# Window attention with a mixture of experts on one core: ScalarE puts the score biases of pairs 1 to 7 into PSUM, and VectorE rounds the third expert

## The chip, the cores and the metric

One core of a Trainium2 chip runs the whole program. The metric is device time in microseconds (us); lower is better. The kernel before has a median of 6585.76 us over 3 runs (6585.39 to 6585.8).

## The reference

The input `x` is 32 images of 56 x 56 tokens with 96 channels. Each image goes through a layer norm, then attention in shifted windows of 7 x 7 tokens (49 tokens, 12 heads of 8 channels), and a residual. Then come a second layer norm and a mixture of 4 experts (96 to 384 to 96, exact gelu, the best 2 of 4 by a softmax gate), and a second residual. The part that the change touches is the bias of the scores and the hidden layer of the experts:

```python
attn = einsum('bhwnqd,bhwnkd->bhwnqk', q, k) * (1.0 / sqrt(hd))
attn = attn + bias        # rel_table[index], one 49 x 49 table per head
attn = attn + mask        # -inf between the two sides of the shift:
                          # last window row and last window column
p = softmax(attn)
...
h = gelu(einsum('bsd,edh->ebsh', x, w1) + b1)
y = einsum('ebsh,ehd->ebsd', h, w2) + b2
```

## The kernel before, in words

The work is cut into 128 units: 4 for each of the 32 images. A unit is two strips of 7 rows by 56 columns, 784 tokens, or 16 windows. Its attention is done in 8 pairs of windows (n = 0 to 7); the two windows of a pair lie on partitions 0 to 48 and 64 to 112, so that an operation on a pair has 113 partitions and 12 heads x 49 = 588 elements.

`step(f, a, b, u)` runs once per unit and engine, and each engine has its own order written out by hand; semaphores tie the engines together. In a step, `f` is the unit whose expert layer is worked on, `a` the next one, whose attention runs beside it, and `b` the one after. A step begins with the hidden layer of `f` (24 matmul groups on TensorE, 24 gelus on ScalarE into `g_sb`). Then `attention(a, b, f)` follows. The first unit's attention stands in the prologue without an `f`, so 127 attentions have expert work between their pairs.

One pair's way through the engines in the kernel before:

- TensorE, `scores` (from L1003): waits until VectorE has read the last pair's scores (`sub_done`), then writes the bias into the two PSUM banks of `ps_s` with four matmuls of a selection matrix against `bias16` (L1016, two column sizes on two halves of the array). For pairs 3 and 7 two more matmuls (L1020) add the mask between rows. Six matmuls (L1026) add q times k.
- VectorE, `softmax_pair`: the maximum over the keys (`s_max`, L735), and the difference (`s_sub`, L739, updates `sub_done`).
- ScalarE, `exps` (L558): the exponent into `p_sb`.
- TensorE, `transpose_p` (L1036): six transposes into `ps_t`.
- ScalarE, `copy_pt` (L563): copies them into `pt_sb`.
- TensorE, `attend` (L1053): 24 small matmuls into `ps_o`. VectorE normalises (`normalise_o`), and TensorE turns the result (`turn_o`, L1062).

In iteration n of its loop TensorE does scores of pair n+1, attend of pair n-1, transposes of pair n, then the expert groups of `GROUPS_AT[n]` (L1116 to L1127, 18 or 27 matmuls with bias), then the turn of pair n-1. ScalarE does the copy of pair n, the exponent of pair n+1, and a rounding out of `ROUND_AT[n]`. In iteration 4 it then saves the first half's output (`save_o`, L574), without which TensorE may not attend pair 4, and rounds the normalised input of unit `b` (`x1_high`, L500).

The experts' matmuls take the gelus as two fp16 parts, `g_hi` (rounded) and `g_lo` (what is left). There are 12 chunks of 128 x 784, three per expert. VectorE rounds chunks 0 to 5 (L873) while the gelus run, ScalarE chunks 6 to 11 (L534) during attention, one in each of iterations 1, 2, 3, 5, 6 and 7, into buffers that chunks 0 to 5 have left. GpSimd (POOL) subtracts the low parts of chunks 3 to 11 (L448).

Of the kernel before, what the change touches and what calls it, by code (L numbers as in the profile page):

```python
# [28 lines left out]
F16 = mybir.dt.float16  # L29
ALU = mybir.AluOpType  # L30
# [5 lines left out]
WW = W * W  # L36
# [46 lines left out]
def piece_list(u, shift):  # L83

    out = []
    for half in range(2):
# [7 lines left out]
        for r0, rows, row in ((0, IMG - shift, shift), (IMG - shift, shift, 0)):  # L94
# [14 lines left out]
ROUND_AT = ((), (6,), (7,), (8,), (), (9,), (10,), (11,))  # L109
# [15 lines left out]
N_ROUND, N_LO = CHUNKS // 2, CHUNKS - CPE  # L125
# [9 lines left out]
         ("rel", HEADS * WW), ("lr", HEADS * WW), ("ul", HEADS * WW), ("sel", SPAN), ("selB", SPAN))  # L135
# [3 lines left out]
def build(nc, x, packed, wp, consts, out, keys):  # L139
    ctx = ExitStack()  # L140
    with ctx:
# [89 lines left out]
        g_hi = sb("g_hi", [128, 2 * CPE, TOK + PAD], F16)  # L231
# [24 lines left out]
        max_done, sub_done = sem("max_done"), sem("sub_done")  # L256
# [150 lines left out]
        def _(pool):  # L407
# [33 lines left out]
            def low_part(f, chunk):  # L441

                if chunk < 2 * CPE:
                    pool.wait_ge(hi_dve, at(f, N_ROUND, chunk + 1))
                else:
                    pool.wait_ge(hi_act, at(f, N_ROUND, chunk - 2 * CPE + 1))
                slot = chunk % (2 * CPE)
                nc.gpsimd.tensor_tensor(g_lo[:, slot, 0:TOK], g_sb[:, chunk, :], g_hi[:, slot, 0:TOK],  # L448
                                        ALU.subtract).then_inc(lo_done, 1)
# [42 lines left out]
        def _(act):  # L492
# [38 lines left out]
            def round_chunk(f, chunk):  # L531

                act.wait_ge(y_done, at(f, N_Y, PARTS * (chunk // CPE - 1)))
                nc.scalar.activation(g_hi[:, chunk - 2 * CPE, 0:TOK], g_sb[:, chunk, :], ACT.Copy  # L534
                                     ).then_inc(hi_act, 1)
# [77 lines left out]
            def step(f, a, b, u):  # L613
                for i in range(8):
                    gelus(f, 3 * i)
                    if i == 0:
                        router_tanh(f)
                if a is not None:
                    load_tables(ACT.Exp)
                    attention(a, b, f)  # L620
                else:
                    for chunk in range(2 * CPE, CHUNKS):
                        round_chunk(f, chunk)
# [5 lines left out]
        def _(dve):  # L629
# [10 lines left out]
            def setup():  # L640
# [8 lines left out]
                fill(V.tensor_copy(selB16[:, :], offs["selB"]))  # L649
                fill(V.tensor_copy(ul16[:, :], offs["ul"]))  # L650
# [18 lines left out]
                fill(V.tensor_copy(tmp, offs["rel"]))  # L669
                for v in range(2):  # L670
                    fill(V.tensor_tensor(bias16[NB:128, v, :], offs["rel"][NB:128, :], tmp[NB:128, :],
                                         ALU.subtract))
                fill(V.tensor_copy(bias16[0:NB, 0, :], tmp[0:NB, :]))
                fill(V.tensor_tensor(bias16[0:NB, 1, :], offs["rel"][0:NB, :], offs["lr"][0:NB, :], ALU.add))
# [265 lines left out]
            def step(f, a, b, u):  # L940
                router_b(f)
                for chunk in range(CPE):
                    round_chunk(f, chunk)
                for chunk in range(CPE):
                    low_part(f, chunk)
                for chunk in range(CPE, 2 * CPE):
                    round_chunk(f, chunk)
                if a is not None:
                    softmax_pair(a, 0)
                    attention(a, b, f)  # L950
                else:
                    for g in range(N_Y):
                        combine(f, g)
# [5 lines left out]
        def _(pe):  # L959
# [143 lines left out]
            def experts(f, g):  # L1103
# [104 lines left out]
def _layout(w_qkv, b_qkv, w_proj, b_proj, rel_table, gate_w, gate_b, w1, b1, w2, b2):  # L1208
# [65 lines left out]
```

## Time and profile before

| what | value |
|---|---|
| median of 3 runs | 6585.76 us |
| the profiled execution | 6582.02 us |
| its span, first to last instruction | 6580.2 us |
| mean granted TensorE clock | 0.996 |
| busy: TensorE, VectorE, ScalarE, GpSimd | 96%, 76%, 72%, 57% |

The span is divided into 128 units of nearly the same length. One unit in the middle, from 3004.7 us on, is read below. PE is TensorE's matmuls, PEld its weight loads, DVE VectorE, ACT ScalarE, POOL GpSimd. Matmuls overlap in the records, so that starts of consecutive pieces say more than durations.

### The profile page before, as it was taken

How to read it: one execution, taken by the hardware profiler on the slowest of the kernel's cores; microseconds unless marked ns; L12 is line 12 of the kernel's file. 1: busy time of each engine (PE TensorE's matmuls, PEld its weight loads, DVE VectorE, ACT ScalarE, POOL GpSimd, SP SyncE). 2: the span in 40 equal slices, each digit the busy share in tenths (PEclk: the TensorE clock that was granted, in tenths of full speed). 3: DMA queues.
4: the chain of work that ended last, by engine and by line, in shares of the span. 5: the costliest groups of instructions: out<-in, count | busy, mean ns of one | idle time of the engine just before them, and what ended most of it. 6: DMA issues, size and time to landing. Idle time of an engine off the chain costs nothing.

```text
span 6580.2 us, 265098 instructions
## 1 busy us (share of the span) xinstructions
PE 6329.5 (96%) x99456; PEld 5075.5 (77%) x99456; DVE 5021.6 (76%) x15655; ACT 4719.7 (72%) x9087; POOL 3763.3 (57%) x3337
## 2 busy tenths in 40 slices
PE   5999999999999999999999999999999999999997
PEld 4777777777777777777777777777777777777776
DVE  5777777777777777777777777777777777777775
ACT  3777777777777777777777777777777777777775
POOL 2565555555555565556555555555565555555555
PEclk9999999999999999999999999999999999999999
DMA  1111111111111111111111111111111111111110
GB/s 57 44 43 44 46 45 43 44 46 44 45 42 46 44 44 44 45 43 44 44 46 43 44 45 45 43 45 45 44 43 45 46 44 43 44 46 45 45 41 24
DMA packets 190611, 290.00 MB, mean 44 GB/s; under 512 B 42450, under 2 KB 151634, under 8 KB 189266
## 3 DMA queue, kind: packets, MB, share of 16 engines
q1 hardware_dynamic: 189394, 273.23, 14.4%
q8 instruction: 831, 13.62, 0.9%
q14 instruction: 386, 3.16, 0.2%
HBM read 138.18 MB, written 77.07 MB: 33 GB/s over the span
## 4 chain that ended last, share of the span: by engine, by line
PE 73%; DVE 15%; issue 5%; ACT 4%; POOL 2%; SPq 1%; DVEq 0%; DMA 0%; ACTq 0%; POOLq 0%
PE ps_t L1036 10%; PE ps_o L1053 9%; PE ps_f L964 8%; PE ps_f L965 8%; PE ps_f L966 8%; PE ps_s L1016 5%; PE ps_s L1026 4%; PE ps_f L1127 3%; PE ps_f L1125 3%; PE ps_f L1123 3%; DVE s_max L735 3%; PE ps_o L1062 3%; POOL rstd L437 2%; DVE stat L766 2%; PE ps_t L983 2%
## 5 line engine op out<-in xcount | busy, mean ns | idle before, releaser
L448 POOL TENSOR_TENSOR g_lo<-g_sb,g_hi 128x784 f16<-128x784 f32 x1152 | 2014.9, 1758 | 1774.3 <-DVE g_hi L873 1013.8
L541 ACT ACTIVATE g_sb<-ps_f 128x392 f32<-128x392 f32 x3072 | 1525.9, 497 | 127.6 <-PE ps_f L966 126.8
L563 ACT ACTIVATE pt_sb<-ps_t 113x588 f32<-113x588 f32 x1024 | 677.4, 662 | 1077.8 <-PE ps_t L1036 1065.0
L735 DVE TENSOR_REDUCE s_max<-ps_s 113x12 f32<-113x588 f32 x1024 | 789.1, 771 | 746.9 <-PE ps_s L1026 746.9
L1127 PE MATMUL ps_f<-w_hi,g_lo 128*128 128x96 f16 x8832 | 1227.3, 206 | 0.0
L1125 PE MATMUL ps_f<-w_lo,g_hi 128*128 128x96 f16 x8832 | 1226.7, 206 | 0.0
L1123 PE MATMUL ps_f<-w_hi,g_hi 128*128 128x96 f16 x8832 | 1226.1, 206 | 0.0
L458 POOL TENSOR_TENSOR xr<-y_gated,xr 112x192 f32<-112x192 f32 (+1 forms) x1536 | 987.0, 660 | 374.6 <-DVE y_gated L891 275.7
L964 PE MATMUL ps_f<-x_hi,w_hi 128*128 128x392 f16 x3072 | 1012.2, 329 | 19.5 <-issue 5.3
L965 PE MATMUL ps_f<-x_lo,w_hi 128*128 128x392 f16 x3072 | 1010.7, 329 | 0.0
L966 PE MATMUL ps_f<-x_hi,w_lo 128*128 128x392 f16 x3072 | 1010.6, 329 | 0.0
L1036 PE MATMUL ps_t<-ident,p_sb 113*113 113x113 f32 x6144 | 854.6, 275 | 26.9 <-ACT p_sb L558 26.7
L1125 PEld LDWEIGHTS ps_f<-w_lo,g_hi 128*128 128x128 f16 x8832 | 862.9, 98 | 10.2
L1123 PEld LDWEIGHTS ps_f<-w_hi,g_hi 128*128 128x128 f16 x8832 | 865.2, 98 | 0.1
L1127 PEld LDWEIGHTS ps_f<-w_hi,g_lo 128*128 128x128 f16 x8832 | 863.5, 98 | 0.0
L739 DVE TENSOR_TENSOR s_sub<-ps_s,s_max 113x588 f32<-113x588 f32 x1024 | 790.0, 772 | 57.0
L1053 PEld LDWEIGHTS ps_o<-v_bd,pt_sb 113*49 113x49 f32 x24576 | 738.0, 125 | 114.1 <-ACT pt_sb L563 67.1
L1053 PE MATMUL ps_o<-v_bd,pt_sb 113*49 113x18 f32 x24576 | 785.5, 198 | 24.2 <-ACT pt_sb L563 20.2
L558 ACT ACTIVATE p_sb<-s_sub 113x588 f32<-113x588 f32 x1024 | 715.7, 699 | 77.6 <-DVE s_sub L739 72.6
L1036 PEld LDWEIGHTS ps_t<-ident,p_sb 113*113 113x113 f32 x6144 | 695.9, 178 | 80.4 <-issue 51.3
L534 ACT ACTIVATE g_hi<-g_sb 128x784 f16<-128x784 f32 x768 | 647.3, 843 | 3.1 <-PE ps_f L1127 3.1
L437 POOL TENSOR_TENSOR rstd<-ve,cst 112x4 f32<-112x4 f32 (+1 forms) x256 | 270.9, 1058 | 595.4 <-DVE ve L775 595.4
(132 smaller groups left out, 13415.6 us busy)
## 6 DMA issues: line engine op xcount, KB each, us to landing
k_bd<-keys SPq DMA_DIRECT2D x1536, 36.8 KB
q_st<-qk_hi SPq DMA_DIRECT2D x768, 49.0 KB, 1.9
xr<-x SPq DMA_DIRECT2D x224, 139.1 KB
out<-xr SPq DMA_DIRECT2D x224, 139.1 KB
xa<-x SPq DMA_DIRECT2D x224, 136.5 KB
keys<-qk_hi SPq DMA_DIRECT2D x128, 147.0 KB, 2.4
keys<-qk_lo SPq DMA_DIRECT2D x128, 147.0 KB, 2.8
q_st<-qk_lo SPq DMA_DIRECT2D x384, 49.0 KB, 2.0
```

Source lines behind the costliest of these rows:

```text
L448: nc.gpsimd.tensor_tensor(g_lo[:, slot, 0:TOK], g_sb[:, chunk, :], g_hi[:, slot, 0:TOK], ALU.subtract).then_inc(lo_done, 1)
L458: nc.gpsimd.tensor_tensor(slot, y_gated[:, g % 4, 0:n * C], slot, ALU.add).then_inc(comb_done, 1)
L541: nc.scalar.activation(g_sb[:, chunk, half * STRIP:(half + 1) * STRIP], h_bank[k % 3][:, 0:STRIP], ACT.Gelu, scale=1.0 / WSCALE).then_inc( ...
L735: V.tensor_reduce(s_max[:, :], scores, AX.X, ALU.max).then_inc(max_done, 1)
L964: T.matmul(outp, lhs_hi, rhs_hi, start=start, stop=False, skip_group_check=True)
L965: T.matmul(outp, lhs_hi, rhs_lo, start=False, stop=False, skip_group_check=True)
L966: return T.matmul(outp, lhs_lo, rhs_hi, start=False, stop=True, skip_group_check=True)
L1036: ins = T.transpose(bank[2 + p // 4][0:SPAN, (p % 4) * 128:(p % 4) * 128 + SPAN], p_sb[0:SPAN, n % 2, 2 * p:2 * p + 2, :].rearrange("p h k ...
L1053: ins = T.matmul(ps_o[NB * s:NB * s + WW, O0 + p * 2 * VW:O0 + (p + 1) * 2 * VW], pt_sb[0:SPAN, p, s * WW:(s + 1) * WW], v_bd[0:SPAN, win ...
L1123: T.matmul(outp, g_hi[:, slot, cols], w2_hi[:, wc], start=False, stop=False, skip_group_check=True)
L1125: T.matmul(outp, g_hi[:, slot, cols], w2_lo[:, wc], start=False, stop=False, skip_group_check=True)
L1127: ins = T.matmul(outp, g_lo[:, slot, cols], w2_hi[:, wc], start=False, stop=(c == CPE - 1), skip_group_check=True)
```

## The change

ScalarE has a new routine `put_bias(a, n)`: it waits until the scores of pair n-1 have been read (`sub_done`), and copies one of four ready bias tables (`biases`, 113 partitions x 588, with the masks already in them) from SBUF into the banks of `ps_s`. TensorE's `scores` has no bias matmuls for pairs 1 to 7 any more; it waits for `bias_done` and adds q times k to what lies there. Pair 0 keeps its four bias matmuls. In ScalarE's order the bias of pair 1 stands ahead of the exponent of pair 0, and in iterations 0 to 5 the bias of pair n+2 ahead of the copy of pair n and the exponent of pair n+1.

VectorE now rounds chunks 6 to 8 too, right after chunks 3 to 5, into three more buffers of `g_hi`; ScalarE rounds only chunks 9 to 11, in iterations 5, 6 and 7. GpSimd's `low_part` waits for the buffer of `g_lo` itself. The tables are set up once: six VectorE instructions go, six come.

```diff
-ROUND_AT = ((), (6,), (7,), (8,), (), (9,), (10,), (11,))
+ROUND_AT = ((), (), (), (), (), (9,), (10,), (11,))
...
-N_ROUND, N_LO = CHUNKS // 2, CHUNKS - CPE
+N_ROUND, N_LO = 3 * CPE, CHUNKS - CPE
...
             def low_part(f, chunk):
 
-                if chunk < 2 * CPE:
+                if chunk < 3 * CPE:
                     pool.wait_ge(hi_dve, at(f, N_ROUND, chunk + 1))
                 else:
-                    pool.wait_ge(hi_act, at(f, N_ROUND, chunk - 2 * CPE + 1))
+                    pool.wait_ge(hi_act, at(f, CPE, chunk - 3 * CPE + 1))
+                if chunk >= 2 * CPE:
+
+                    pool.wait_ge(y_done, at(f, N_Y, PARTS * (chunk // CPE - 1)))
...
+            def put_bias(a, n):
+
+                act.wait_ge(sub_done, at(a, N_S, n))
+                half, wr = n // 4, 2 * (n % 4)
+                variant = (1 if half == 1 and a[1] % UPI == UPI - 1 else 0) + (2 if wr == NW - 2 else 0)
+                nc.scalar.activation(ps_s[0:SPAN, 0:HEADS * NB].rearrange("p (h k) -> p h k", k=NB)[:, :, 0:WW],
+                                     biases[:, variant, :].rearrange("p (h k) -> p h k", k=WW), ACT.Copy
+                                     ).then_inc(bias_done, 1)
...
             def attention(a, b, f=None):
 
+                put_bias(a, 1)
                 exps(a, 0)
                 for n in range(8):
                     if n == 7 and b is not None:
                         qk_high(b, 0)
+                    if n < 6:
+                        put_bias(a, n + 2)
                     copy_pt(a, n)
...
-                for chunk in range(CPE, 2 * CPE):
+                for chunk in range(CPE, 3 * CPE):
                     round_chunk(f, chunk)
...
                 else:
-                    pe.wait_ge(sub_done, at(a, N_S, n))
-                variant = 1 if half == 1 and a[1] % UPI == UPI - 1 else 0
+                    pe.wait_ge(bias_done, at(a, N_S - 1, n))
                 s3 = ps_s[:, 0:HEADS * NB].rearrange("p (h k) -> p h k", k=NB)
-                blocks = ((slice(0, NB), slice(0, NB)), (slice(NB, SPAN), slice(NB, SPAN)))
-                for h0, h1 in ((0, 8), (8, 12)):
-                    for rows, cols in blocks:
-                        T.matmul(s3[rows, h0:h1, 0:WW], sel16[:, cols], bias16[:, variant, h0 * WW:h1 * WW],
-                                 start=True, stop=False, skip_group_check=True)
-                    if wr == NW - 2:
-                        rows, cols = blocks[1]
-                        T.matmul(s3[rows, h0:h1, 0:WW], selB16[:, cols], ul16[:, h0 * WW:h1 * WW],
-                                 start=False, stop=False, skip_group_check=True)
+                if n == 0:
+                    for h0, h1 in ((0, 8), (8, 12)):
+                        for r0 in (0, NB):
+                            T.matmul(s3[r0:min(r0 + NB, SPAN), h0:h1, 0:WW], sel16[:, r0:min(r0 + NB, SPAN)],
+                                     bias16[:, h0 * WW:h1 * WW], start=True, stop=False, skip_group_check=True)
```

ScalarE's order at the head of an attention before (`p_sb<-s_sub` is an exponent, `pt_sb<-ps_t` a copy: exponent and copy of pair 0, then of pair 1; in brackets stand the semaphores waited for, and an ISA row is a wait by itself):

```order
101 L557 ISA [waits sub_done]
102 L558 ACTIVATE p_sb<-s_sub 113x12x49 [waits pt_done]
103 L562 REGISTER_ALU
104 L563 ACTIVATE pt_sb<-ps_t 113x588 [waits pt_done]
105 L552 REGISTER_ALU
106 L558 ACTIVATE p_sb<-s_sub 113x12x49 [waits pt_done,sub_done]
107 L562 REGISTER_ALU
108 L563 ACTIVATE pt_sb<-ps_t 113x588 [waits pt_done]
```

The same place in the changed kernel (`ps_s<-biases` is the new copy, of pairs 1, 2 and 3):

```order
108 L559 ACTIVATE ps_s<-biases 113x12x49 [waits sub_done]
109 L569 ISA [waits sub_done]
110 L570 ACTIVATE p_sb<-s_sub 113x12x49 [waits pt_done]
111 L556 REGISTER_ALU
112 L559 ACTIVATE ps_s<-biases 113x12x49 [waits sub_done]
113 L574 REGISTER_ALU
114 L575 ACTIVATE pt_sb<-ps_t 113x588 [waits pt_done]
115 L570 ACTIVATE p_sb<-s_sub 113x12x49 [waits pt_done,sub_done]
116 L556 REGISTER_ALU
117 L559 ACTIVATE ps_s<-biases 113x12x49 [waits sub_done]
```

Each copy of transposes now stands behind a bias that waits for VectorE's difference of the next pair; before, it waited for TensorE's transposes alone.

TensorE's order at the scores of pair 1 before (`ps_s<-bias,sel` are bias matmuls, `ps_s<-k_bd,q_st` q times k, `ps_t<-ident,p_sb` transposes):

```order
334 L1016 MATMUL ps_s<-bias,sel 64x8x49 [waits sub_done]
335 L1016 MATMUL ps_s<-bias,sel 49x8x49
336 L1016 MATMUL ps_s<-bias,sel 64x4x49
337 L1016 MATMUL ps_s<-bias,sel 49x4x49
338 L1026 MATMUL ps_s<-k_bd,q_st 49x4x49 x6
339 L1033 REGISTER_ALU
340 L1036 MATMUL ps_t<-ident,p_sb 113x113 [waits exp_done,v_saved]
```

And in the changed kernel:

```order
309 L1035 MATMUL ps_s<-k_bd,q_st 49x4x49 [waits bias_done]
310 L1035 MATMUL ps_s<-k_bd,q_st 49x4x49 x5
311 L1042 ISA
312 L1043 REGISTER_ALU [waits v_saved]
313 L1045 MATMUL ps_t<-ident,p_sb 113x113 [waits exp_done]
```

The four bias matmuls are gone, and the six that stay wait for ScalarE in place of VectorE.

## Rows read from the trace of the kernel before

**Rows 1.** The page, part 1: busy time and share of each engine.

```profile
PE 6329.5 (96%) x99456; PEld 5075.5 (77%) x99456; DVE 5021.6 (76%) x15655; ACT 4719.7 (72%) x9087; POOL 3763.3 (57%) x3337
```

**Rows 2.** The page, part 4: the chain that ended last, by engine.

```profile
PE 73%; DVE 15%; issue 5%; ACT 4%; POOL 2%; SPq 1%; DVEq 0%; DMA 0%; ACTq 0%; POOLq 0%
```

**Rows 3.** Busy time by stretch: an attention; stretch, its length, then engines.

```profile
3004.70:3034.00 29.30, 28.78 (x566) 25.51 (x566) 22.23 (x62) 19.11 (x34) 20.93 (x18) 1.00 0.10 31
```

**Rows 4.** Timeline of PE, same unit: start, length, instruction, [idle before <-releaser].

```profile
3008.08 0.42 PE L1036 MATMUL ps_t<-ident,p_sb 113*113 113x113 f32 x2 [0.21 <-ACT p_sb L558]
...
3010.10 0.44 PE L1016 MATMUL ps_s<-bias,sel 128*64 128x392 f16 x4
3010.38 0.43 PE L1026 MATMUL ps_s<-k_bd,q_st 128*49 128x196 f16 x6
...
3011.25 0.35 PE L1036 MATMUL ps_t<-ident,p_sb 113*113 113x113 f32 x1
...
3013.14 0.36 PE L1016 MATMUL ps_s<-bias,sel 128*64 128x392 f16 x2
...
3014.55 0.35 PE L1036 MATMUL ps_t<-ident,p_sb 113*113 113x113 f32 x1
...
3017.58 0.35 PE L1036 MATMUL ps_t<-ident,p_sb 113*113 113x113 f32 x1
...
3019.74 0.45 PE L1016 MATMUL ps_s<-bias,sel 128*64 128x392 f16 x4
...
3020.89 0.35 PE L1036 MATMUL ps_t<-ident,p_sb 113*113 113x113 f32 x1
...
3022.78 0.44 PE L1016 MATMUL ps_s<-bias,sel 128*64 128x392 f16 x4
...
3023.51 0.73 PE L1053 MATMUL ps_o<-v_bd,pt_sb 113*49 113x18 f32 x24
3024.17 0.35 PE L1036 MATMUL ps_t<-ident,p_sb 113*113 113x113 f32 x1
...
3025.90 0.36 PE L1016 MATMUL ps_s<-bias,sel 128*64 128x392 f16 x2
...
3027.31 0.45 PE L1036 MATMUL ps_t<-ident,p_sb 113*113 113x113 f32 x2
```

**Rows 5.** Timeline of ACT, end of the gelus and that attention.

```profile
2999.83 5.47 ACT L541 ACTIVATE g_sb<-ps_f 128x392 f32<-128x392 f32 x11
...
3007.23 0.71 ACT L558 ACTIVATE p_sb<-s_sub 113x588 f32<-113x588 f32 x1 [0.41 <-DVE s_sub L739]
...
3012.14 0.66 ACT L563 ACTIVATE pt_sb<-ps_t 113x588 f32<-113x588 f32 x1 [1.82 <-PE ps_t L1036]
3012.70 0.69 ACT L558 ACTIVATE p_sb<-s_sub 113x588 f32<-113x588 f32 x1
...
3022.97 0.49 ACT L574 ACTIVATE o_sb<-ps_o 96x392 f32<-96x392 f32 x1
3023.36 1.05 ACT L500 ACTIVATE x_hi<-ps_f 96x224 f16<-96x224 f32 x4
```

**Rows 6.** Timeline of DVE, end of the gelus and that attention.

```profile
3001.33 1.51 DVE L873 CAST g_hi<-g_sb 128x784 f16<-128x784 f32 x3
3005.45 0.77 DVE L735 TENSOR_REDUCE s_max<-ps_s 113x12 f32<-113x588 f32 x1 [2.60 <-PE ps_s L1026]
3006.34 0.77 DVE L739 TENSOR_TENSOR s_sub<-ps_s,s_max 113x588 f32<-113x588 f32 x1
...
3010.85 0.77 DVE L735 TENSOR_REDUCE s_max<-ps_s 113x12 f32<-113x588 f32 x1 [0.19 <-PE ps_s L1026]
3011.65 0.77 DVE L739 TENSOR_TENSOR s_sub<-ps_s,s_max 113x588 f32<-113x588 f32 x1
...
3055.84 0.77 DVE L735 TENSOR_REDUCE s_max<-ps_s 113x12 f32<-113x588 f32 x1 [2.53 <-PE ps_s L1026]
```

**Rows 7.** Timeline of POOL, the low parts of chunks 3 to 5.

```profile
3001.97 5.68 POOL L448 TENSOR_TENSOR g_lo<-g_sb,g_hi 128x784 f16<-128x784 f32 x3 [7.70 <-DVE g_hi L873]
```

More of the change, by code:

```diff
@@ L134 @@
          ("w2", CHUNKS * C),
-         ("rel", HEADS * WW), ("lr", HEADS * WW), ("ul", HEADS * WW), ("sel", SPAN), ("selB", SPAN))
+         ("rel", HEADS * WW), ("lr", HEADS * WW), ("ul", HEADS * WW), ("sel", SPAN))
 N_CONST = 5
@@ L168, in build @@
         sel16 = sb("sel16", [128, SPAN], F16)
-        selB16 = sb("selB16", [128, SPAN], F16)
-        ul16 = sb("ul16", [128, HEADS * WW], F16)
-        bias16 = sb("bias16", [128, 2, HEADS * WW], F16)
+        bias16 = sb("bias16", [128, HEADS * WW], F16)
+        biases = sb("biases", [SPAN, 4, HEADS * WW])
         wqk_hi = sb("wqk_hi", [128, 2 * C], F16)
@@ L230, in build @@
         g_sb = sb("g_sb", [128, CHUNKS, TOK])
-        g_hi = sb("g_hi", [128, 2 * CPE, TOK + PAD], F16)
+        g_hi = sb("g_hi", [128, 3 * CPE, TOK + PAD], F16)
         g_lo = sb("g_lo", [128, 2 * CPE, TOK + PAD], F16)
@@ L255, in build @@
         k_out = [sem("khi_out"), sem("klo_out")]
-        max_done, sub_done = sem("max_done"), sem("sub_done")
+        max_done, sub_done, bias_done = sem("max_done"), sem("sub_done"), sem("bias_done")
         rec_done = sem("rec_done")
@@ L441, in low_part @@
             def low_part(f, chunk):
-                if chunk < 2 * CPE:
+                if chunk < 3 * CPE:
                     pool.wait_ge(hi_dve, at(f, N_ROUND, chunk + 1))
                 else:
-                    pool.wait_ge(hi_act, at(f, N_ROUND, chunk - 2 * CPE + 1))
+                    pool.wait_ge(hi_act, at(f, CPE, chunk - 3 * CPE + 1))
+                if chunk >= 2 * CPE:
+                    pool.wait_ge(y_done, at(f, N_Y, PARTS * (chunk // CPE - 1)))
                 slot = chunk % (2 * CPE)
-                nc.gpsimd.tensor_tensor(g_lo[:, slot, 0:TOK], g_sb[:, chunk, :], g_hi[:, slot, 0:TOK],
+                nc.gpsimd.tensor_tensor(g_lo[:, slot, 0:TOK], g_sb[:, chunk, :],
+                                        g_hi[:, chunk % (3 * CPE), 0:TOK],
                                         ALU.subtract).then_inc(lo_done, 1)
@@ L533, in round_chunk @@
                 act.wait_ge(y_done, at(f, N_Y, PARTS * (chunk // CPE - 1)))
-                nc.scalar.activation(g_hi[:, chunk - 2 * CPE, 0:TOK], g_sb[:, chunk, :], ACT.Copy
+                nc.scalar.activation(g_hi[:, chunk - 3 * CPE, 0:TOK], g_sb[:, chunk, :], ACT.Copy
                                      ).then_inc(hi_act, 1)
@@ L621, in step @@
                 else:
-                    for chunk in range(2 * CPE, CHUNKS):
+                    for chunk in range(3 * CPE, CHUNKS):
                         round_chunk(f, chunk)
@@ L648, in setup @@
                 fill(V.tensor_copy(sel16[:, :], offs["sel"]))
-                fill(V.tensor_copy(selB16[:, :], offs["selB"]))
-                fill(V.tensor_copy(ul16[:, :], offs["ul"]))
                 for src, hi, lo in (("wqk", wqk_hi, wqk_lo), ("wv", wv_hi, wv_lo),
@@ L669, in setup @@
                 fill(V.tensor_copy(tmp, offs["rel"]))
+                fill(V.tensor_tensor(bias16[NB:128, :], offs["rel"][NB:128, :], tmp[NB:128, :], ALU.subtract))
+                fill(V.tensor_copy(bias16[0:NB, :], tmp[0:NB, :]))
+                fill(V.tensor_copy(biases[:, 0, :], offs["rel"][0:SPAN, :]))
+                fill(V.tensor_tensor(biases[:, 1, :], biases[:, 0, :], offs["lr"][0:SPAN, :], ALU.add))
                 for v in range(2):
[L671 to L674, printed above, removed]
+                    fill(V.tensor_tensor(biases[:, 2 + v, :], biases[:, v, :], offs["ul"][0:SPAN, :], ALU.add))
                 fill(V.memset(q_st[C:128, :, :], 0.0))
@@ L1120, in experts @@
                     for c in range(CPE):
-                        slot, wc = e % 2 * CPE + c, slice((e * CPE + c) * C, (e * CPE + c + 1) * C)
+                        hi, lo = e % 3 * CPE + c, e % 2 * CPE + c
+                        wc = slice((e * CPE + c) * C, (e * CPE + c + 1) * C)
                         outp = y[:, k * C:(k + 1) * C]
-                        T.matmul(outp, g_hi[:, slot, cols], w2_hi[:, wc], start=False, stop=False,
+                        T.matmul(outp, g_hi[:, hi, cols], w2_hi[:, wc], start=False, stop=False,
                                  skip_group_check=True)
-                        T.matmul(outp, g_hi[:, slot, cols], w2_lo[:, wc], start=False, stop=False,
+                        T.matmul(outp, g_hi[:, hi, cols], w2_lo[:, wc], start=False, stop=False,
                                  skip_group_check=True)
-                        ins = T.matmul(outp, g_lo[:, slot, cols], w2_hi[:, wc], start=False,
+                        ins = T.matmul(outp, g_lo[:, lo, cols], w2_hi[:, wc], start=False,
                                        stop=(c == CPE - 1), skip_group_check=True)
@@ L1223, in _layout @@
     lr, ul = np.zeros((128, HEADS, WW), f), np.zeros((128, HEADS, WW), f)
-    lr[0:WW] = np.where(late(col)[:, None] != late(col)[None], MASKED, 0.0)[:, None, :]
-    ul[0:WW] = np.where(late(row)[:, None] != late(row)[None], MASKED, 0.0)[:, None, :]
-    sel, selB = np.zeros((128, SPAN), f), np.zeros((128, SPAN), f)
+    lr[0:WW] = lr[NB:SPAN] = np.where(late(col)[:, None] != late(col)[None], MASKED, 0.0)[:, None, :]
+    ul[NB:SPAN] = np.where(late(row)[:, None] != late(row)[None], MASKED, 0.0)[:, None, :]
+    sel = np.zeros((128, SPAN), f)
     q = np.arange(WW)
@@ L1230, in _layout @@
             sel[k0 + q, m0 + q] = 1.0
-    selB[q, NB + q] = 1.0
     parts = {"wqk": _rows(wqk), "wv": _rows(wv), "wg": _rows(wg), "w1": _rows(w1b), "b2": b2r,
              "rel": rel.reshape(128, -1), "lr": lr.reshape(128, -1), "ul": ul.reshape(128, -1),
-             "sel": sel, "selB": selB}
+             "sel": sel}
     parts["w2"] = w2.reshape(EXPERTS, CPE, 128, C).transpose(2, 0, 1, 3).reshape(128, CHUNKS * C)
```

## The prediction

> **What bounds the kernel now.** I read the page first. TensorE is busy 96% of the span, VectorE 76%, ScalarE 72% [rows 1], and the chain that ended last lies 73% on TensorE [rows 2]. Taking work from TensorE looks right. But 15% of that chain is VectorE and 4% ScalarE, so there are places where TensorE waits for a softmax. The busy time by stretch puts the change in its stage: an attention takes 29.30 us of a unit's 50.39 (3005.45 to 3055.84 on VectorE), and TensorE is busy in 28.78 of them [rows 3, 6]. There is hardly a gap, because its order was laid out so that each wait ends just in time. The question is whether the waits still end in time when TensorE's part shrinks and ScalarE's grows. So I went through one unit, engine by engine [rows 4 to 6], and asked of each pair what ends last.
>
> From these rows I take the lengths of the links:
> - Scores to the end of the difference: the scores of pair 2 start at 3010.38, its maximum at 3010.85 (0.47), the difference 0.80 later, for 0.77: 2.04 together. For pairs 0 and 1 maximum and difference start 0.89 apart (3005.45, 3006.34), which makes 2.13 [rows 4, 6].
> - The difference ends at 3007.11, ScalarE starts at 3007.23: 0.12. The exponent starts 0.85 before its transposes (3007.23, 3008.08). ScalarE starts an exponent 0.56 after a copy (3012.14, 3012.70) [rows 4 to 6].
> - On TensorE, scores to transposes takes 0.87 (3010.38, 3011.25), attend to transposes 0.66 (3023.51, 3024.17). From transposes to the next scores it takes 2.02 (3008.08 to 3010.10), 1.89 (3011.25 to 3013.14, and 3020.89 to 3022.78), 2.16 with three expert tiles (3017.58 to 3019.74), and 1.73 (3024.17 to 3025.90) [rows 4].
>
> **The change part by part.** *TensorE loses* the bias matmuls: 0.28 per pair (3010.10 to 3010.38), and 0.26 more for pairs 3 and 7, since bias to transposes is 1.41 for pair 3 (3013.14 to 3014.55) and 1.15 for pair 2 (3010.10 to 3011.25) [rows 4]. That is 7 x 0.28 + 2 x 0.26 = 2.48 us per unit, 315 us over 127 units, if nothing else ended later.
>
> *ScalarE gains* seven copies per unit of 113 x 588. Their price isn't in the trace, since ScalarE writes to no PSUM bank there. The nearest rows are the copy of the same size out of PSUM, 0.66, and the exponent from SBUF to SBUF, 0.71 [rows 5]. For the lower end: 392 elements take 5.47 / 11 = 0.497 [rows 5], so 588 cost 0.49 for elements and 0.17 for the rest; a third off the rest gives 0.60. I take 0.66, a copy with PSUM on one side, and 0.60 to 0.71 for the range. The Trainium skill (ScalarE: Activation LUTs, Step-by-step: what each stage is for) calls PSUM the faster destination of the two for ScalarE; no row here shows it, and by it the sum would lie near the lower end, worked out below. From a ScalarE end to TensorE's start it is 0.14 (3007.94 to 3008.08) or 0.05 (3023.46 to 3023.51) [rows 4, 5]; I take 0.10, and either end shifts the result by 0.05 per unit at most.
>
> *The new wait.* A bias needs the old scores read, so scores now follow the difference by 0.12 + 0.66 + 0.10 = 0.88, and a new round stands there: scores, maximum, difference, bias, scores, 2.92 us. Queued behind the waiting bias on ScalarE are the copy of transposes (0.56 later) and the exponent (1.12 later), and TensorE waits for both. Transposes come at bias + 1.12 + 0.85 = bias + 1.97, or scores + 0.87. Times before in brackets [rows 4]:
> - Head: bias 1 starts at 3007.23, where exponent 0 stood. Scores 1 at 3007.99, exponent 0 at 3007.79, transposes 0 at 3008.64 (3008.08). TensorE stands still ahead of scores 1.
> - Scores 1 + 2.13 + 0.12: bias 2 at 3010.24, scores 2 at 3011.00 (TensorE alone: 3010.66), transposes 1 at 3012.21 (3011.25): **0.96 late**.
> - Bias 3 at 3013.16; scores 3 when TensorE is free, 3014.10; transposes 2 at 3015.13 (3014.55): 0.58. Here the mask matmuls pay.
> - Bias 4 at 3016.26, scores 4 at 3017.02, transposes 3 at 3018.23 (3017.58): 0.65.
> - Scores 5 at 3020.39 (TensorE), transposes 4 at 3021.26 (3020.89): 0.37.
> - Iteration 4: bias 6 at 3020.39 + 2.16 = 3022.55, scores 6 at 3023.31. Copy 4, exponent 5 and `save_o` follow, so `save_o` starts at 3022.55 + 3 x 0.56 = 3024.23 (3022.97 [rows 5]). Attend 4 needs it: 0.54 later, 3024.77 (3023.51); transposes 5 at 3025.43 (3024.17): **1.26 late**.
> - Behind `save_o` come 0.39 and the 1.05 of `x1_high` [rows 5], then bias 7 at 3025.67. TensorE reaches scores 7 at 3025.43 + 1.73 = 3027.16; transposes 6 at 3028.03 (3027.31): **0.72 late**.
>
> No bias follows in iterations 6 and 7, and all later work is as before, so a unit ends 0.72 later. Per pair the gain and the new round nearly cancel (2.92 against periods of 3.03 to 3.31 of the transposes); the head and iteration 4 are what is lost. The sum: 0.72 x 127 = 91 us, on the profiled execution's 6582.0, 6673. The median of the runs is 3.7 above that execution, so I say **6677**. The same steps with 0.60 for the copy end 0.48 late (61 us, 6647), with 0.71 they end 0.92 late (117 us, 6703).
>
> *Roundings.* Three leave ScalarE in iterations 1 to 3, where it stood idle for 1.82 ahead of a copy [rows 5]: nothing on the path. VectorE gets three casts, 1.51, where it waits 2.60 for the scores of pair 0 [rows 6]. Their gelus are done: the 18th by 2999.83 + 5 x 0.497 = 3002.3 [rows 5], and the earlier casts end at 3002.84. So they end at 3004.35, with 1.1 left; without that cover each microsecond would fall on the head. GpSimd's low parts of chunks 3 to 5 end at 3007.65 [rows 7]; pushed back by all of 1.51 they still end 3 us before expert group 3, which needs them behind transposes 1. Set-up swaps six instructions for six: nothing.
>
> **The rivals.**
> - *A, ScalarE's queue does not hold the copies: faster.* TensorE stays the bound behind the head. Then 0.96 is lost and pairs 3 to 7 save 5 x 0.28 + 2 x 0.26 = 1.92: 0.96 gained per unit, 122 us, **6464**. For it speaks TensorE's 96% [rows 1]. It decides where a bias has ended before the copy's own transposes: before, copy 1 started at 3012.14, while the difference that bias 3 needs ended at 3012.42, so the bias would end at 3013.2, 1.06 too late [rows 5, 6]. Chance 0.13.
> - *B, `save_o` isn't pushed back.* If turn and save still come first in time, transposes 5 stand at 3022.55 + 1.97 = 3024.52, scores 7 at 3026.25, transposes 6 at bias 7 (3025.47) + 1.97 = 3027.44, only 0.13 late: 17 us, **6602**. Against it stands ScalarE's strict order, for it that my links are single readings. Chance 0.12.
> - *C, the casts come late.* If one waits for one of GpSimd's subtractions (5.68 / 3 = 1.89 [rows 7]), the 1.1 left are gone and the head is 0.8 later: some 100 us more, **6780**. Against it: three casts took 1.51 with GpSimd at work from 3001.97 on [rows 6, 7]. The Trainium skill (SBUF — State Buffer, Who interferes with whom) says that a VectorE cast in a two-port mode and a GpSimd instruction shut each other out for a whole instruction, whoever comes first; in this trace the casts that met GpSimd show no such wait. Chance 0.05.
>
> **How the numbers follow.** The forecast has the other 0.70, and its own range is 6647 to 6703. About 0.2% (13 us) can be told from no change. Faster: A and 0.02 of B, 0.15. Same: 0.06 of B and 0.05 of a forecast whose links are all a little shorter, 0.11. Slower: the rest, 0.74. The range reaches down past B to 6575 and up to 6740, between the forecast's upper end and C; A and C stay out, 0.18.
>
> **What would show it.** In the changed profile: 896 ScalarE copies into `ps_s` of 0.60 to 0.71; ScalarE's idle time ahead of them ended by VectorE's difference, and hardly any ahead of the copies out of `ps_t`; transposes late by 0.6, 1.0, 0.6, 0.65, 0.4, 1.3 and 0.7 against the first maximum of the unit; `save_o` 1.3 later; TensorE with idle time ahead of scores, attend and transposes. I am wrong if copies of transposes still start on TensorE's word, if a unit's stretch behind pair 6 changes by itself, or if the first maximum comes more than 2.6 behind the end of chunk 5's cast.

## The result, and the profile after

The changed kernel takes **6685.1 us** (median of 4 runs, 6682.8 to 6686.7) beside 6585.8 for the kernel before: a ratio of 1.0150 [1.0133, 1.0168], 1.5% slower. Forecast were 6677 and a range of 6575 to 6740. The profiled execution took 6686.55 us, with a span of 6684.7 at a mean granted clock of 0.983; before, the span was 6580.2 at 0.996. So 104.5 us came on top, and the clock fell as well.

The changed kernel's page, parts 1 and 4, beside [rows 1, 2]:

```profile
PE 6165.4 (92%) x95360; PEld 4871.9 (73%) x95360; DVE 5261.3 (79%) x16039; ACT 4933.5 (74%) x9599; POOL 3941.3 (59%) x3337
...
PE 59%; DVE 22%; ACT 9%; issue 7%; POOL 2%; ACTq 0%; DVEq 0%; DMA 0%; SPq 0%; POOLq 0%
```

TensorE lost 4096 bias matmuls and is busy 164 us less, but of the chain it has 59% in place of 73%; VectorE and ScalarE took what it gave up, 7 and 5 points. Part 5 of its page, the copies of biases, the copies of transposes and the attends (busy us, mean ns of one, then the idle time ahead of them and what ended it):

```profile
L559 ACT ACTIVATE ps_s<-biases 113x588 f32<-113x588 f32 x896 | 601.3, 671 | 864.4 <-DVE s_sub L753 864.4
L575 ACT ACTIVATE pt_sb<-ps_t 113x588 f32<-113x588 f32 x1024 | 665.3, 650 | 173.9 <-PE ps_t L1045 151.4
L1062 PE MATMUL ps_o<-v_bd,pt_sb 113*49 113x18 f32 x24576 | 743.4, 200 | 193.5 <-ACT o_sb L586 139.4
```

ScalarE waits 864 us for VectorE's differences, and little for transposes any more (151 us, before 1065). TensorE waits 139 us for `save_o`, ahead of attend 4. These are the waits that the prediction put there.

One unit on ScalarE (timeline; its first maximum, VectorE's of pair 0, from which times in a unit are counted here, is at 3208.24):

```profile
3209.95 0.67 ACT L559 ACTIVATE ps_s<-biases 113x588 f32<-113x588 f32 x1 [0.33 <-DVE s_sub L753]
3210.55 0.69 ACT L570 ACTIVATE p_sb<-s_sub 113x588 f32<-113x588 f32 x1
...
3212.85 0.67 ACT L559 ACTIVATE ps_s<-biases 113x588 f32<-113x588 f32 x1 [1.62 <-DVE s_sub L753]
3213.45 0.64 ACT L575 ACTIVATE pt_sb<-ps_t 113x588 f32<-113x588 f32 x1
3213.99 0.69 ACT L570 ACTIVATE p_sb<-s_sub 113x588 f32<-113x588 f32 x1
...
3224.84 0.67 ACT L559 ACTIVATE ps_s<-biases 113x588 f32<-113x588 f32 x1 [1.55 <-DVE s_sub L753]
3225.44 0.64 ACT L575 ACTIVATE pt_sb<-ps_t 113x588 f32<-113x588 f32 x1
3225.98 0.69 ACT L570 ACTIVATE p_sb<-s_sub 113x588 f32<-113x588 f32 x1
3226.57 0.47 ACT L586 ACTIVATE o_sb<-ps_o 96x392 f32<-96x392 f32 x1
```

Bias, copy and exponent stand in a row, and `save_o` behind the bias of pair 6: 18.33 after the first maximum, where it was 17.52 before [rows 5, 6]. TensorE in the same unit (timeline, the scores, attends and transposes that are used below):

```profile
3210.66 0.44 PE L1035 MATMUL ps_s<-k_bd,q_st 128*49 128x196 f16 x6 [0.66 <-ACT ps_s L559]
3211.29 0.85 PE L1045 MATMUL ps_t<-ident,p_sb 113*113 113x113 f32 x6 [0.18 <-ACT p_sb L570]
...
3214.81 0.85 PE L1045 MATMUL ps_t<-ident,p_sb 113*113 113x113 f32 x6
...
3216.53 0.44 PE L1035 MATMUL ps_s<-k_bd,q_st 128*49 128x196 f16 x6
...
3225.55 0.45 PE L1035 MATMUL ps_s<-k_bd,q_st 128*49 128x196 f16 x6
...
3227.09 0.73 PE L1062 MATMUL ps_o<-v_bd,pt_sb 113*49 113x18 f32 x24 [1.09 <-ACT o_sb L586]
3227.76 0.85 PE L1045 MATMUL ps_t<-ident,p_sb 113*113 113x113 f32 x6
...
3230.38 0.85 PE L1045 MATMUL ps_t<-ident,p_sb 113*113 113x113 f32 x6
```

TensorE stands still 0.66 us ahead of the scores of pair 1 and 1.09 ahead of attend 4; before, no pause of it between 300 and 6300 us is longer than 0.35. Now VectorE's first maximum of five units, and the end of the gelus (timeline), and units by stretch (windows; columns: stretch, its length, the busy time of PE, PEld, DVE, ACT and POOL, granted clock, DMA share, GB/s):

```profile
3052.79 0.77 DVE L749 TENSOR_REDUCE s_max<-ps_s 113x12 f32<-113x588 f32 x1 [1.16 <-PE ps_s L1035]
...
3104.99 0.77 DVE L749 TENSOR_REDUCE s_max<-ps_s 113x12 f32<-113x588 f32 x1 [1.16 <-PE ps_s L1035]
...
3155.67 0.77 DVE L749 TENSOR_REDUCE s_max<-ps_s 113x12 f32<-113x588 f32 x1 [1.16 <-PE ps_s L1035]
...
3204.57 2.95 DVE L887 CAST g_hi<-g_sb 128x784 f16<-128x784 f32 x6
3208.24 0.77 DVE L749 TENSOR_REDUCE s_max<-ps_s 113x12 f32<-113x588 f32 x1 [0.72 <-PE ps_s L1035]
3209.14 0.77 DVE L753 TENSOR_TENSOR s_sub<-ps_s,s_max 113x588 f32<-113x588 f32 x1
...
3258.92 0.77 DVE L749 TENSOR_REDUCE s_max<-ps_s 113x12 f32<-113x588 f32 x1 [1.16 <-PE ps_s L1035]
```

```profile
3052.79:3104.99 52.20, 48.99 (x747) 38.89 (x746) 40.90 (x126) 38.53 (x76) 30.71 (x27) 0.97 0.15 43
3104.99:3155.67 50.68, 47.47 (x747) 37.45 (x746) 40.90 (x125) 38.53 (x76) 30.70 (x27) 1.00 0.16 44
3072.70:3075.90 3.20, 3.20 (x35) 2.94 (x36) 1.20 (x4) 2.36 (x4) 0.23 (x1) 0.50 0.05 21
```

There are two kinds of units. Most take 50.68 us, 0.28 more than the 50.40 before; they are called undisturbed below. Others take 52.2: inside them lies a stretch of some 3.4 us in which the granted clock is 0.50, TensorE's lower level of 1.2 GHz, while the rest of the unit has 2.4 GHz. It sets in 0.4 to 1.0 us behind the start of attend 4 in every one of them, and transposes 6 are the first that come late by it (23.70 behind the first maximum in place of 22.14). The middle of the program, from the first maximum of unit 2 to that of unit 124, holds 34 such units, two to four units apart; before, it held none. The unit that holds the loop's jump back, one in four, is 0.32 longer with either kernel (51.00, before 50.73), and 52.57 with such a stretch in it (3155.67 to 3208.24).

**Where the 104.5 us are.** The middle grew by 87.0: 122 x 0.28 = 34 over all units, and the other 53 in the 34 with the low clock, 1.55 each. The start (up to unit 2) grew by 8.3 and the end by 9.2; in both the clock stands low for longer than before (51 us in one piece at the start, 27 before); why, no run tests. So about a third is the new waits, half the clock in the middle, and the rest the two ends.

### The profile page after: what moved, and what is told of

Read it like the earlier page. It is cut to its first block, busy times and chain, and to the rows that moved or that the text cites. A ratio compares the mean times of both kernels' runs of the same rounds, so it can differ in the third digit from the quotient of the medians.

```text
span 6684.7 us, 259934 instructions
## 1 busy us (share of the span) xinstructions
PE 6165.4 (92%) x95360; PEld 4871.9 (73%) x95360; DVE 5261.3 (79%) x16039; ACT 4933.5 (74%) x9599; POOL 3941.3 (59%) x3337
## 4 chain that ended last, share of the span: by engine, by line
PE 59%; DVE 22%; ACT 9%; issue 7%; POOL 2%; ACTq 0%; DVEq 0%; DMA 0%; SPq 0%; POOLq 0%
PE ps_f L978 8%; PE ps_o L1062 8%; PE ps_f L980 8%; PE ps_f L979 8%; PE ps_t L1045 8%; DVE s_max L749 6%; DVE s_sub L753 6%; ACT pt_sb L575 4%; PE ps_s L1035 4%; PE ps_f L1137 2%; PE ps_f L1135 2%; PE ps_f L1133 2%; POOL rstd L436 2%; DVE stat L780 2%; PE ps_t L997 2%
## 5 line engine op out<-in xcount | busy, mean ns | idle before, releaser
L450 POOL TENSOR_TENSOR g_lo<-g_sb,g_hi 128x784 f16<-128x784 f32 x1152 | 2198.8, 1917 | 1818.0 <-DVE g_hi L887 1013.6
L1137 PE MATMUL ps_f<-w_hi,g_lo 128*128 128x96 f16 x8832 | 1253.6, 208 | 0.0
L1135 PE MATMUL ps_f<-w_lo,g_hi 128*128 128x96 f16 x8832 | 1252.9, 208 | 0.0
L1133 PE MATMUL ps_f<-w_hi,g_hi 128*128 128x96 f16 x8832 | 1252.6, 208 | 0.0
L559 ACT ACTIVATE ps_s<-biases 113x588 f32<-113x588 f32 x896 | 601.3, 671 | 864.4 <-DVE s_sub L753 864.4
L1062 PEld LDWEIGHTS ps_o<-v_bd,pt_sb 113*49 113x49 f32 x24576 | 664.4, 126 | 371.0 <-ACT pt_sb L575 188.2
L1062 PE MATMUL ps_o<-v_bd,pt_sb 113*49 113x18 f32 x24576 | 743.4, 200 | 193.5 <-ACT o_sb L586 139.4
L1045 PE MATMUL ps_t<-ident,p_sb 113*113 113x113 f32 x6144 | 884.2, 282 | 23.2 <-ACT p_sb L570 23.2
L1045 PEld LDWEIGHTS ps_t<-ident,p_sb 113*113 113x113 f32 x6144 | 718.0, 183 | 80.7 <-ACT p_sb L570 50.8
L905 DVE TENSOR_TENSOR y_gated<-ps_f,gate 112x192 f32<-112x192 f32 (+1 forms) x1280 | 480.0, 383 | 220.5 <-PE ps_f L1137 197.4
```

The source lines that it names most:

```text
L1045: ins = T.transpose(bank[2 + p // 4][0:SPAN, (p % 4) * 128:(p % 4) * 128 + SPAN], p_sb[0:SPAN, n % 2, 2 * p:2 * p + 2, :].rearrange("p h k ...
L1062: ins = T.matmul(ps_o[NB * s:NB * s + WW, O0 + p * 2 * VW:O0 + (p + 1) * 2 * VW], pt_sb[0:SPAN, p, s * WW:(s + 1) * WW], v_bd[0:SPAN, win ...
L1133: T.matmul(outp, g_hi[:, hi, cols], w2_hi[:, wc], start=False, stop=False, skip_group_check=True)
L1135: T.matmul(outp, g_hi[:, hi, cols], w2_lo[:, wc], start=False, stop=False, skip_group_check=True)
L1137: ins = T.matmul(outp, g_lo[:, lo, cols], w2_hi[:, wc], start=False, stop=(c == CPE - 1), skip_group_check=True)
```

## Experiments

Each result is the median in us, then its ratio to the kernel before, measured beside it, with a 95% interval.

The theory after the result: the reordering of ScalarE costs the 0.28 per unit, and the pause ahead of attend 4 that it makes brings the clock down. The rivals: the rounding costs something or makes the room; the clock falls because TensorE has less to do, wherever its pauses lie.

**The rounding alone.** Kernel before, with the third expert rounded on VectorE, biases as before.

```diff
-ROUND_AT = ((), (6,), (7,), (8,), (), (9,), (10,), (11,))
+ROUND_AT = ((), (), (), (), (), (9,), (10,), (11,))
...
-                for chunk in range(CPE, 2 * CPE):
+                for chunk in range(CPE, 3 * CPE):
                     round_chunk(f, chunk)
```

> Kernel before with only the third expert's rounding moved to VectorE; the biases stay matmuls on TensorE. My theory (the time goes into two waits of ScalarE's queue, at the head of an attention and behind bias 6, and into TensorE's clock, which falls after the second): the casts lie in VectorE's idle time, so within 0.2% of before, 6573 to 6599 us, granted clock 0.99 or more. Rival, the casts come late or hold GpSimd up: a first maximum of a unit later than before by 0.3 us or more, 6625 us or more.

Measured: 6613.4, 1.0041 [1.0027, 1.0056], outside what was expected. Yet three units in four are as before (50.41), and every transpose of theirs within 0.02. All of it lies in the fourth, with the jump back: 51.60 in place of 50.73, 0.87 x 32 = 28 us. There ScalarE's first gelu comes late. The changed order of the rounding first, its unit's first maximum at 3121.16; then the kernel before, first maximum 3106.24 (timelines of ScalarE):

```profile
3160.92 1.27 ACT L545 ACTIVATE g_sb<-ps_f 128x392 f32<-128x392 f32 x3 [2.35 <-PE ps_f L970]
```

```profile
3143.98 1.00 ACT L541 ACTIVATE g_sb<-ps_f 128x392 f32<-128x392 f32 x2 [0.33 <-PE ps_f L966]
```

That is 39.76 behind the first maximum in place of 37.74, with the idle time 2.0 longer. The profile names TensorE's tile, which also was the releaser before.

**The same with three tiny instructions.** Where ScalarE's three roundings stood, it now copies one element each, so that its program has its old length again.

```diff
                         for chunk in ROUND_AT[n]:
                             round_chunk(f, chunk)
+                        if 1 <= n <= 3:
+                            nc.scalar.activation(tiny[:, n - 1:n], cst[0:1, 4:5], ACT.Copy)
```

> The rounding-only kernel with three ScalarE copies of one element where its three roundings stood, so that ScalarE's part of the loop has as many engine instructions as before. If its 0.4% came from the jump back of ScalarE's shorter loop (once in four units the first gelu starts 2 us late), the delay goes: units at the jump of 50.7 us, 6580 to 6597 us. Rival, it comes from the moved rounding itself: 6605 to 6620 us as without the copies.

Measured: 6586.0, 1.0003 [0.9994, 1.0013]; the units with the jump are back at 50.73. So moving the rounding costs nothing, as forecast, and the 28 us of the run above went with the number of ScalarE's instructions. What ScalarE does in those 2 us no run shows. The changed kernel has other counts again; its unit with the jump is longer than the others by no more than before (0.32 and 0.33).

**The biases alone.** Changed kernel, chunks 6 to 8 rounded by ScalarE.

```diff
-ROUND_AT = ((), (), (), (), (), (9,), (10,), (11,))
+ROUND_AT = ((), (6,), (7,), (8,), (), (9,), (10,), (11,))
...
-                for chunk in range(CPE, 3 * CPE):
+                for chunk in range(CPE, 2 * CPE):
                     round_chunk(f, chunk)
```

> The changed kernel with ScalarE rounding chunks 6 to 8 in iterations 1 to 3 as before; only the biases are moved. My theory: ScalarE has room in those iterations, so the time of the changed kernel, 6672 to 6699 us, with the clock falling in about one unit of four. Rival, the moved rounding is what costs: near the time before, 6573 to 6599 us. Rival, the roundings are what made room on ScalarE: 6750 us or more.

Measured: 6680.1, 1.0144 [1.0127, 1.0161]; undisturbed units 50.68, and 33 of the units 4 to 123 with the low clock (34 in the changed kernel). The loss is the biases', and the moved rounding buys nothing here.

**The pause filled.** Changed kernel, with six needless matmuls into a bank that is free there, between the scores of pair 6 and attend 4.

```diff
                         scores(a, n + 1)
+                    if n == 5 and f is not None:
+                        for _ in range(6):
+                            T.matmul(bank[7][:, 0:STRIP], w1_hi[:, 0:128], x2_hi[:, 0:STRIP], start=True,
+                                     stop=True, skip_group_check=True)
                     if n:
                         attend(a, n - 1)
```

> The changed kernel with six needless matmuls of 128x392 on TensorE between scores 6 and attend 4, in the time in which it waits for save_o (they write a bank that nobody reads until it is written again). My theory says that the clock falls because TensorE stands still there: units stay at 50.7 us, none is 1.57 us longer, granted clock 0.99 or more, 6620 to 6645 us. Rival, the clock falls for another reason (other idle places, fewer matmuls in the whole attention): 6675 to 6700 us as the changed kernel. Rival, the matmuls themselves delay attend 4: 6700 us or more.

Measured: 6624.0, 1.0058 [1.0041, 1.0074]. Its timelines of TensorE and of VectorE's first maxima, one unit:

```profile
3248.70 1.17 PE L1163 MATMUL ps_f<-x_hi,w_hi 128*128 128x392 f16 x6
3249.86 0.73 PE L1062 MATMUL ps_o<-v_bd,pt_sb 113*49 113x18 f32 x24
```

```profile
3231.01 0.77 DVE L749 TENSOR_REDUCE s_max<-ps_s 113x12 f32<-113x588 f32 x1 [1.15 <-PE ps_s L1035]
...
3281.69 0.77 DVE L749 TENSOR_REDUCE s_max<-ps_s 113x12 f32<-113x588 f32 x1 [1.16 <-PE ps_s L1035]
```

Attend 4 starts no earlier (18.85 behind the first maximum, as in the changed kernel), every unit still takes 50.68, and no unit from 4 to 123 holds a stretch of low clock any more. Work that nobody needs takes 61 us off. This is the price of the clock, shown by itself. Of the 38 us that remain, 35 are the middle's, 0.28 a unit for the new waits; the rest lies mostly at the start.

**The kernel before, with a pause.** Two needless copies on ScalarE (128 x 784 and 128 x 392, 1.26 us by its timeline) ahead of `save_o`; all bias matmuls stay.

```diff
                     if n == 4:
+                        if f is not None:
+                            for j, k in enumerate((TOK, STRIP)):
+                                nc.scalar.activation(spare[:, j, 0:k], g_sb[:, 9, 0:k], ACT.Copy)
                         save_o(a, 0)
```

> The kernel before, all its bias matmuls kept, with two needless ScalarE copies (128x784 and 128x392, into a spare buffer) in front of save_o in iteration 4, so that TensorE stands still ahead of attend 4 for some 1.3 us, as in the changed kernel. Theory that standing still there brings the clock down: drops to 1.2 GHz appear, units without one 1.0 to 1.3 us longer than before, those with one 1.5 us more, about 6750 to 6800 us. Rival, the clock falls in the changed kernel because TensorE has fewer matmuls: no drop here, 6700 to 6750 us, granted clock 0.995 or more.

One run: 6765.1. TensorE (timeline) and the stretch behind it (windows):

```profile
3470.08 0.73 PE L1057 MATMUL ps_o<-v_bd,pt_sb 113*49 113x18 f32 x24 [1.13 <-ACT o_sb L575]
3470.74 1.36 PE L1040 MATMUL ps_t<-ident,p_sb 113*113 113x113 f32 x6
```

```profile
3471.00:3474.20 3.20, 3.20 (x30) 2.81 (x31) 1.30 (x5) 1.99 (x3) 0.00 (x0) 0.50 0.09 30
```

A pause of 1.13 us makes the undisturbed units 1.11 longer (51.51) and brings the low clock to 25 units, 1.58 longer still. The kernel before is thus sensitive too, and nothing was added to it but the two copies that make the pause. That less work on TensorE as such brings the clock down is refuted by this and the run above.

**Pair 1's bias back on TensorE.** Changed kernel; ScalarE writes the biases of pairs 2 to 7.

```diff
-                put_bias(a, 1)
                 exps(a, 0)
...
+                elif n == 1:
+                    pe.wait_ge(sub_done, at(a, N_S, n))
                 else:
-                    pe.wait_ge(bias_done, at(a, N_S - 1, n))
+                    pe.wait_ge(bias_done, at(a, N_S - 2, n - 1))
...
-                if n == 0:
+                if n < 2:
                     for h0, h1 in ((0, 8), (8, 12)):
```

> The changed kernel with the biases of pair 1 as matmuls on TensorE again (as pair 0's), so that nothing stands in front of exponent 0. My theory: the head's loss goes (transposes 0 as before, transposes 1 at most 0.4 us late in place of 0.75), iteration 4 and its fall of the clock stay: undisturbed units of 50.2 to 50.4 us, one unit of about four 1.57 us longer, 6620 to 6650 us. Rival, the head costs nothing because TensorE has other slack: 6675 to 6700 us.

Measured: 6679.6, 1.0146 [1.0131, 1.0162], a miss. The undisturbed units are 50.24, as expected (the head costs 0.44 a unit), but now 70 units from 4 to 123 hold a stretch of low clock, not 34, at 1.50 each on average (1.34 to 1.63). Two units by VectorE's first maximum (timeline), the second with the low clock, and TensorE ahead of attend 4 in each:

```profile
3256.07 0.77 DVE L748 TENSOR_REDUCE s_max<-ps_s 113x12 f32<-113x588 f32 x1 [1.17 <-PE ps_s L1036]
...
3306.32 0.77 DVE L748 TENSOR_REDUCE s_max<-ps_s 113x12 f32<-113x588 f32 x1 [1.16 <-PE ps_s L1036]
...
3357.93 0.77 DVE L748 TENSOR_REDUCE s_max<-ps_s 113x12 f32<-113x588 f32 x1 [1.17 <-PE ps_s L1036]
```

```profile
3274.49 0.73 PE L1063 MATMUL ps_o<-v_bd,pt_sb 113*49 113x18 f32 x24 [1.09 <-ACT o_sb L586]
...
3324.73 0.73 PE L1063 MATMUL ps_o<-v_bd,pt_sb 113*49 113x18 f32 x24 [1.10 <-ACT o_sb L586]
```

The pause is the same in both. So a pause of this length makes the fall possible; which units it strikes, and why more of them here, the runs leave open.

**The same, with the pause filled** by the six matmuls shown above.

> Pair 1's biases on TensorE, and the six needless matmuls between scores 6 and attend 4. If that run was slow only by its falls of the clock, they go here and every unit takes the 50.24 us of its undisturbed ones: 6560 to 6585 us, at or a little below the time before. Rival, the clock falls somewhere else once this place is filled: 6620 us or more.

Measured: 6568.2 (9 runs), 0.9975 [0.9965, 0.9986], units of 50.24 and none with the low clock: 111 us below the run above, for added work. The miss was the clock, not the step on pair 1.

**`save_o` before the exponent.** Changed kernel; iteration 4 runs copy 4, bias 6, `save_o`, exponent 5.

```diff
-                    if n < 6:
-                        put_bias(a, n + 2)
-                    copy_pt(a, n)
+                    if n == 4:
+                        copy_pt(a, n)
+                        put_bias(a, n + 2)
+                        save_o(a, 0)
+                    else:
+                        if n < 6:
+                            put_bias(a, n + 2)
+                        copy_pt(a, n)
...
-                    if n == 4:
-                        save_o(a, 0)
-                        if b is not None:
-                            x1_high(b)
+                    if n == 4 and b is not None:
+                        x1_high(b)
```

> The changed kernel with ScalarE's iteration 4 in another order: copy 4, bias 6, save_o, exponent 5 (in place of bias 6, copy 4, exponent 5, save_o). My theory: transposes 5 move from 0.8 us behind those of before to 0.1 behind, transposes 6 to 0.2 ahead, the clock stays up though no matmul is added; units of 50.1 to 50.2 us, 6545 to 6575 us. Rival, every pair pays the longer round of scores, difference and bias, so that later pairs lose it again: 6620 us or more. Rival, the clock falls because the attention holds fewer matmuls: drops stay, 6600 us or more.

Measured: 6538.5, 0.9931 [0.9914, 0.9947], a little better than expected and faster than the kernel before. Units of 49.98, none with the low clock; transposes 5 to 7 come 0.06, 0.26 and 0.42 earlier than before the change. One order in one iteration turns the sign.

**Both, and copy 0 ahead of bias 2.** Pair 1's bias on TensorE, iteration 4 as above, and in iteration 0, against the run above:

```diff
+                        if n == 0:
+                            copy_pt(a, n)
                         if n < 6:
                             put_bias(a, n + 2)
-                        copy_pt(a, n)
+                        if n:
+                            copy_pt(a, n)
```

> Both repairs: pair 1 on TensorE, copy 0 in front of bias 2, and iteration 4 as copy 4, bias 6, save_o, exponent 5. If the two waits and the clock are all that the changed kernel lost, TensorE's saved matmuls now show: units of 49.2 to 49.6 us, no fall of the clock in the middle, 6430 to 6490 us, faster than both kernels by over 1%. Rival, the round of scores, difference and bias (2.81 us) binds every pair: no better than the run with iteration 4 alone, 6525 us or more.

Measured: **6462.3** (5 runs), 0.9814 [0.9801, 0.9828]: 1.9% faster than the kernel before, 3.3% faster than the changed one. Timelines of ScalarE and of TensorE in iteration 4, and of two first maxima on VectorE:

```profile
3218.10 0.66 ACT L575 ACTIVATE pt_sb<-ps_t 113x588 f32<-113x588 f32 x1 [1.08 <-PE ps_t L1052]
3218.66 0.66 ACT L559 ACTIVATE ps_s<-biases 113x588 f32<-113x588 f32 x1
3219.29 0.49 ACT L586 ACTIVATE o_sb<-ps_o 96x392 f32<-96x392 f32 x1
3219.68 0.69 ACT L570 ACTIVATE p_sb<-s_sub 113x588 f32<-113x588 f32 x1
```

```profile
3219.37 0.45 PE L1042 MATMUL ps_s<-k_bd,q_st 128*49 128x196 f16 x6 [0.20 <-ACT ps_s L559]
3219.84 0.73 PE L1069 MATMUL ps_o<-v_bd,pt_sb 113*49 113x18 f32 x24
```

```profile
3202.41 0.77 DVE L754 TENSOR_REDUCE s_max<-ps_s 113x12 f32<-113x588 f32 x1 [1.15 <-PE ps_s L1042]
...
3251.81 0.77 DVE L754 TENSOR_REDUCE s_max<-ps_s 113x12 f32<-113x588 f32 x1 [1.16 <-PE ps_s L1042]
```

Attend 4 follows the scores of pair 6 with no pause, the unit takes 49.40, and the clock stays up. Most copies of biases wait for a difference here too (488 us in all, 864 in the changed kernel), but no longer at the two places where that held TensorE up.

## Why the prediction was right, and where its steps were not

The sign and its reason held: scores now follow difference and bias, ScalarE's strict queue carries the wait on to copy, exponent and `save_o`, and what TensorE saves is lost at the head and in iteration 4 (0.44 and 0.70 a unit, by the runs that take each away). That the total came out 8 us from the forecast is luck: the new waits were put too high, and a cost that no step had, the clock, filled the gap.

**The new round** (forecast 2.92) was over-sized. Transposes of undisturbed units against the first maximum, beside the times of before:

```
transposes of pair     0     1     2     3     4      5     6     7
before              2.63  5.81  9.10 12.14 15.45  18.72 21.86 24.94
after               3.04  6.56  9.38 12.34 15.39  19.51 22.14 25.22
later by            0.41  0.75  0.27  0.21 -0.05   0.78  0.27  0.28
forecast            0.56  0.96  0.58  0.65  0.37   1.26  0.72
```

The shape is the forecast's, pair by pair, and each value lies below it by more and more up to pair 3, by 0.4 to 0.5 from there on. The term that failed is "the difference ends at 3007.11, ScalarE starts at 3007.23: 0.12". It was taken from an exponent and set in front of a copy. The copy starts 0.04 after the difference ends for pair 1 (3209.14 + 0.77 to 3209.95), and 0.03 for pair 2. With that, 0.08 to 0.09 goes from each of four rounds. A second link was too long: from transposes 1 to the scores of pair 3 TensorE takes 1.72 (3214.81 to 3216.53), where 1.89 had been read, and that comes off from transposes 3 on. From ScalarE's end to the scores it takes 0.04 (3210.62 to 3210.66), not 0.10. The exponent's link to its transposes is also shorter than the 0.85 taken: 0.74 at pair 0, 0.82 at pair 1. The remaining links held: bias to transposes 1.96 (3212.85 to 3214.81, forecast 1.97), bias to copy and copy to exponent 0.60 and 0.54 (forecast 0.56 each), transposes 5 to transposes 6 2.62 (forecast 1.73 + 0.87 = 2.60).

**`save_o`** was pushed back by 0.8, not by 1.26, for the same reason, and attend 4 and transposes 5 with it. So a unit loses 0.28, not 0.72: some 36 us over 127 units, not 91. With 0.28 in the forecast's sum (6582.0 + 36 + 3.7) the kernel would have taken some 6622; the run with the pause filled took 6624.

**The clock** was in no step and in no rival. The prediction saw that TensorE would stand still ahead of attend 4 and charged the pause itself. It did not ask what the pause does to the granted clock, though the row of windows gave 1.00 for the attention [rows 3]. That was the larger part, 53 us in the middle.

**ScalarE's copy into a bank** takes 0.67, on the value chosen (0.66, range 0.60 to 0.71). The Trainium skill (ScalarE: Activation LUTs, Step-by-step: what each stage is for) calls PSUM the faster destination; here the 671 ns into PSUM stand beside 650 out of it, and 0.69 for an exponent from SBUF to SBUF, 0.02 at most in its favour, where the lower end of the range needed 0.06.

**Roundings**: nothing on the path, as said. The six casts end at 3207.52 and VectorE still waits 0.72 for the scores there and 1.16 in the other units (forecast 1.1). GpSimd's low parts of chunks 3 to 5 were pushed back inside the bound of 1.51 (timeline of POOL; 5.68 before [rows 7]):

```profile
3255.46 7.11 POOL L450 TENSOR_TENSOR g_lo<-g_sb,g_hi 128x784 f16<-128x784 f32 x3 [7.70 <-DVE g_hi L887]
```

The added 1.43 fell on GpSimd, about what the three added casts take; a cast of VectorE takes 0.49, as before. What the prediction quoted of the Trainium skill (SBUF — State Buffer, Who interferes with whom) may lie behind GpSimd's part, which no run takes apart, but it did no harm.

**The rivals.** *A, faster,* needed ScalarE's queue not to hold the copies of transposes. It does hold them: ScalarE waits 864 us ahead of the biases, and the copy behind one starts 0.60 after it. That two changes of order, with pair 1's bias back on TensorE, gave 6462 beside A's 6464 is chance in the figure, though it shows that the time was there to be had. *B, `save_o` not pushed back,* is false as a mechanism, yet its 0.13 a unit lies nearer to the 0.28 measured than the forecast's 0.72. *C, casts late,* did not come.

## What to carry to other kernels

When work moves from a busy engine to one with a strict queue, list who stands behind the new wait and move the most urgent of them ahead of it; here the order of four instructions in one iteration decided between 1.5% slower and 0.7% faster. Price a new pause of TensorE twice: its length, and what the clock takes behind it, which can be more. A link between two engines is taken from the same kind of instruction in the same kind of place, and one that recurs in every round is worth reading more than once.

## What the runs showed of the hardware

- A pause of 1.09 to 1.13 us in each unit, on a TensorE that was busy 92 to 94% of the span, was followed in some units by 3.4 us at 1.2 GHz, and the unit then took 1.3 to 1.6 us longer. Among the units from 4 to 123, 34 were struck in the changed kernel (33 with all its roundings back on ScalarE), 70 with pair 1's bias on TensorE, 25 in the kernel before with a pause added, and none in any run without that pause. The 0.66 us ahead of the scores of pair 1 stayed in every unit with the pause filled and with `save_o` earlier, and brought none.
- Three one-element instructions more or fewer on ScalarE moved its first gelu behind the loop's jump by 2.0 us, 28 us in all. The cause is open.
